# A new order of all engines' instructions, another bank map and another form of the mask in a fused decoder layer with a routed feed-forward part

## The reference

```
x = x + attn(layernorm(x))              # 16 heads of 8, no mask takes effect; attn itself adds its input again
x = x + xattn(layernorm(x), ctx, ctx)   # 16 heads of 64, RoPE on q and k,
                                        # scores * 64**-0.5, kept where (j <= i) & (j >= i - 32), else -1e30
x = x + ffn(layernorm(x))               # router picks 1 of 8 experts by argmax, plus a shared expert
# expert: silu(x @ gate.T) * (x @ up.T) @ down.T, hidden size 256
```

## Time and profile before

| | |
|---|---|
| median of three runs | 804.68 us (804.55 to 804.92) |
| profiled execution, its own time | 806.58 us |
| profiled execution, span from first to last instruction | 804.8 us |
| TensorE matmul busy | 760.4 us, 94% |
| VectorE busy | 531.7 us, 66% |
| ScalarE busy | 537.5 us, 67% |
| GpSimd busy | 536.5 us, 67% |
| mean busy share of the DMA engines | 25% |
| mean granted TensorE clock | 0.984 of full speed |

### The profile page before, as it was taken

The page is one execution under the profiler, slowest core; times in us unless marked ns, Lnnn a source line. Parts: engine busy times, 40 slices in busy tenths (PEclk is TensorE's granted clock), DMA queues, the critical chain, the costliest instruction groups (busy, mean ns, idle before and its releaser), DMA issues. The chain is left out here.

```text
span 804.8 us, 27623 instructions
## 1 busy us (share of the span) xinstructions
PE 760.4 (94%) x9852; PEld 623.1 (77%) x9852; DVE 531.7 (66%) x1350; ACT 537.5 (67%) x1900; POOL 536.5 (67%) x864
## 2 busy tenths in 40 slices
PE   4889999999999999999999999999899999998893
PEld 2668888888888888888888888888678777876552
DVE  3566776777777767777777767777866685555652
ACT  2367777777777777777777777777577566656451
POOL 4366777777777777777777777777575755565543
PEclk9799999999999999999999999999999999999997
DMA  6031233323222222221111122223150202333230
GB/s 234 8 119 64 91 91 91 91 83 90 89 91 71 70 72 71 70 68 59 60 58 58 67 71 71 71 71 127 68 151 3 81 24 83 103 102 105 69 101 12
DMA packets 56789, 64.01 MB, mean 80 GB/s; under 512 B 4015, under 2 KB 52917, under 8 KB 56657
## 3 DMA queue, kind: packets, MB, share of 16 engines
q1 hardware_dynamic: 52928, 54.06, 21.0%
q0 software_dynamic: 3008, 6.57, 2.4%
q10 hardware_dynamic: 720, 1.62, 0.5%
HBM read 17.79 MB, written 45.35 MB: 78 GB/s over the span
## 5 line engine op out<-in xcount | busy, mean ns | idle before, releaser
L789 ACT ACTIVATE PX<-P,mx 128x128 f32<-128x128 f32 x512 | 183.5, 409 | 67.5 <-DVE mx L559 67.5
L559 DVE TENSOR_REDUCE mx<-P 128x4 f32<-128x512 f32 x128 | 83.1, 674 | 155.4 <-PE P L298 155.4
L956 POOL TENSOR_TENSOR PX<-PX,mx 128x512 f32<-128x512 f32 x128 | 133.2, 1042 | 14.0 <-DVE mx L564 13.9
L789 ACT ACTIVATION_READ_ACCUMULATOR PX<-P,mx 128x1 f32 x512 | 127.2, 248 | 0.0
L951 POOL TENSOR_TENSOR rq<-rq,tq 128x1024 f32<-128x1024 f32 x32 | 75.6, 2363 | 60.5 <-DVE rq L523 60.5
L753 ACT ACTIVATE PS<-P 128x512 f32<-128x512 f32 x128 | 70.6, 607 | 24.9 <-PE P L219 24.9
L498 DVE TENSOR_REDUCE nmf<-P 128x4 f32<-128x512 f32 x128 | 81.3, 679 | 7.0 <-PE P L198 4.2
L798 ACT ACTIVATE PT<-P 128x512 f32<-128x512 f32 x128 | 76.5, 597 | 8.2 <-PE P L307 5.7
L307 PE MATMUL P<-c,PX 128*128 128x128 f32 x512 | 79.3, 278 | 0.0
L307 PEld LDWEIGHTS P<-c,PX 128*128 128x128 f32 x512 | 57.4, 142 | 24.1 <-issue 22.7
L946 POOL TENSOR_TENSOR rk<-rk,tk 128x1024 f32<-128x1024 f32 x32 | 75.5, 2359 | 0.0
(11 more groups left out here) (140 smaller groups left out, 1767.5 us busy)
## 6 DMA issues: line engine op xcount, KB each, us to landing
z_xs<-c SPq DMA_DIRECT2D x34, 1088.0 KB, 5.2
xrow<-z_xs SPq DMA_DIRECT2D x46, 136.0 KB, 3.3
ew<-in_ew SPq DMA_DIRECT2D x9, 384.0 KB, 3.8
x<-in_x SPq DMA_DIRECT2D x32, 64.0 KB, 1.8
cxT<-in_ctxT SPq DMA_DIRECT2D x31, 64.0 KB
out<-yst,xrow POOLq DMA_INDIRECT x46
wk<-in_wk SPq DMA_DIRECT2D x1, 512.0 KB, 4.5
wvT<-in_wvT SPq DMA_DIRECT2D x1, 512.0 KB, 7.1
```

The source lines that it names most:

```text
L559: dve.tensor_reduce(mx[b % 3][:, 0, r, :], v3(bank(f"ds{r}")), AX.X, ALU.max, negate=True).then_inc(S["v_dm"][r], 1)
L789: t = act.activation(PX[(4 * b + r) % 6][:, c, :], p[:, c * 128:c * 128 + 128], ACT.Exp, bias=m[:, 0, r, c:c + 1], scale=1.0, accum_out=m[ ...
L956: pool.tensor_tensor(X[:, :, :], X[:, :, :], mx[b % 3][:, 2, r, :].rearrange("p (h a) -> p h a", a=1).to_broadcast([128, 4, 128]), ALU.mul ...
```

## The change

Three things change. First, the order of the calls in the loops of all five engines; in part a stage is also moved to the turn before or after. The stages and what they compute stay as they are. Second, `BANK`, the map from slots to banks. Third, the mask of `d_s`: it is now written by slices of 32 keys. Sixteen matmuls (four slices for each of four banks) each multiply 32 rows of the transposed mask (`far`) with a 32 x 32 identity (`eye`), repeated for four heads, and write 128 x (4 x 32) elements. The constant `cb` grows from 1296 to 1328 columns.

The bank map and the mask:

```diff
-BANK = dict(a=2, cnt=5, dn=4, dpv0=4, dpv1=6, ds0=3, ds1=2, ds2=7, ds3=1, dt0=2, dt1=0, dt2=1, dt3=7, et=6, gu=0,
-            kE=3, kO=2, ln=7, nmt=2, oT=0, po=4, pos=0, qE=4, qO=5, qkv=1, rt=6, s0=7, s1=0, s2=5, s3=4, st0=5, st1=0,
-            st2=3, st3=6, v0=6, v1=1, wo=5, x1=3, xg0=5, xg1=4, xg2=3, xg3=0, xgt0=1, xgt1=2, xgt2=3, xr0=1, xr1=2,
-            xr2=7, xr3=0, xrt0=4, xrt1=5, xt0=3, xt1=4, xt2=7, xt3=6, xtt0=0, xy0=6, xy1=6, xy2=7, xy3=5, xyt0=6,
+BANK = dict(a=3, cnt=7, dn=1, dpv0=0, dpv1=3, ds0=0, ds1=3, ds2=4, ds3=1, dt0=7, dt1=1, dt2=0, dt3=2, et=6, gu=1,
+            kE=6, kO=6, ln=4, nmt=7, oT=2, po=6, pos=4, qE=3, qO=5, qkv=5, rt=6, s0=2, s1=3, s2=5, s3=0, st0=7, st1=6,
+            st2=2, st3=5, v0=2, v1=7, wo=7, x1=7, xg0=6, xg1=2, xg2=4, xg3=3, xgt0=1, xgt1=2, xgt2=3, xr0=1, xr1=5,
+            xr2=6, xr3=3, xrt0=4, xrt1=5, xt0=0, xt1=0, xt2=5, xt3=3, xtt0=0, xy0=2, xy1=2, xy2=1, xy3=7, xyt0=6,
             xyt1=7)
...
-        rows, cols = (cb[:, 784 + 256 * k:1040 + 256 * k].bitcast(BF16).rearrange("p (h n) -> p h n", h=2) for k in range(2))
+        far, eye = cb[:, 784:1296].bitcast(BF16).rearrange("p (w q) -> p w q", w=4), cb[:, 1296:1328].bitcast(BF16)
...
-                for h in range(2):
+                for w in range(4):
                     for r in range(4):
-                        pe.matmul(v3(p[r]), rows[32 * r:32 * r + 32, h, :],
-                                  cols[32 * r:32 * r + 32, h, :].rearrange("p (a k) -> p a k", a=1).to_broadcast([32, 4, 128]),
-                                  start=(h == 0), stop=False, skip_group_check=True)
+                        pe.matmul(v3(p[r])[:, :, 32 * w:32 * w + 32], far[32 * r:32 * r + 32, w, :],
+                                  eye[32 * r:32 * r + 32, :].rearrange("p (a k) -> p a k", a=1).to_broadcast([32, 4, 32]),
+                                  start=(w == 0), stop=False, skip_group_check=True)
```

On VectorE, in the part of the turn that the text speaks of:

```diff
+                batch(f_y, s - 8)
...
+                batch(b_max, s - 4, 1)
                 batch(b_max, s - 4, 2)
                 batch(b_max, s - 4, 0)
...
+                batch(f_pos, s - 8)
...
+                batch(r_q1, s - 5)
                 batch(r_q3, s - 5)
...
-                batch(d_max, s - 5, 2)
-                batch(f_pos, s - 7)
```

Before, `f_pos` is the last call of VectorE's turn, and `d_y`, `b_cn` and `f_y` open the next. On ScalarE the middle of the turn:

```diff
                 batch(b_nmT, s - 5)
+                batch(d_ox, s - 7, 0)
+                batch(d_ox, s - 7, 1)
+                batch(b_ps, s - 5, 0)
+                batch(b_ps, s - 5, 1)
+                batch(b_ps, s - 5, 2)
+                batch(b_ps, s - 5, 3)
+                batch(a_norm, s - 2)
                 batch(d_exp, s - 6, 1)
                 batch(b_oT, s - 5)
                 batch(d_exp, s - 6, 0)
+                batch(d_exp, s - 6, 3)
...
+                batch(a_q, s - 4)
                 batch(b_cnT, s - 5)
```

```diff
                 weights(s)
-                tile(next_r, s - 33, 0)
-                batch(clear, s - 6)
-                batch(first_r, s - 8)
-                batch(next_cx, s - 4)
+                batch(first_r, s - 9)
+                tile(next_r, s - 34, 0)
                 tile(next_r, s - 34, 1)
                 tile(next_r, s - 34, 2)
+                batch(next_cx, s - 4)
+                batch(next_x, s - 3)
                 tile(next_r, s - 34, 3)
-                batch(next_x, s - 2)
+                batch(clear, s - 6)
```

More of the change, by code:

```diff
@@ L68, in build @@
         c1 = sb("c1", [128, 646])
-        cb = sb("cb", [128, 1296], U16)
+        cb = sb("cb", [128, 1328], U16)
         c2 = sb("c2", [128, C2])
@@ L405, in _ @@
             for s in range(PERIODS):
[L406 to L414, removed]
-                batch(c_v, s - 4, 1)
-                tile(x_dn, s - 33, 1)
-                tile(x_up, s - 32, 0)
-                tile(x_hT, s - 33, 3)
+                batch(b_ln, s - 5)
@@ L419, in _ @@
+                batch(c_v, s - 4, 1)
+                tile(x_tr, s - 32, 2)
+                tile(x_dn, s - 33, 2)
+                batch(f_pos, s - 8)
+                tile(x_up, s - 32, 1)
+                batch(r_q, s - 5, 0)
+                tile(x_dn, s - 33, 3)
+                tile(x_hT, s - 32, 0)
                 batch(e_tr, s - 7)
[L420 to L423, removed]
+                batch(r_q, s - 5, 1)
@@ L424, in _ @@
+                tile(x_up, s - 32, 2)
+                batch(d_t, s - 6, 2)
+                tile(x_tr, s - 32, 3)
                 batch(f_up, s - 7)
[L425 to L434, removed]
@@ L435, in _ @@
-                batch(a_qkv, s - 3)
-                tile(x_dn, s - 33, 3)
                 batch(d_t, s - 6, 3)
                 tile(x_hT, s - 32, 1)
-                batch(b_st, s - 4)
+                batch(b_nm, s - 4)
                 batch(d_pv, s - 6, 0)
                 batch(d_pv, s - 6, 1)
+                batch(b_st, s - 4)
                 batch(d_s, s - 5)
                 batch(b_pv, s - 4)
-                batch(f_pos, s - 7)
+                tile(x_dn, s - 32, 0)
                 batch(d_wo, s - 6)
@@ L446, in _ @@
                 batch(b_oT, s - 4)
-                batch(f_dn, s - 7)
-                batch(r_k, s - 3, 1)
-                tile(x_dn, s - 32, 0)
+                batch(r_k, s - 3, 1)
+                tile(x_up, s - 32, 3)
+                batch(a_qkv, s - 3)
+                batch(b_cn, s - 4)
+                batch(c_v, s - 3, 0)
+                tile(x_hT, s - 32, 2)
+                tile(x_tr, s - 31, 0)
+                batch(a_tr, s - 1)
+                batch(b_x1, s - 4)
+                batch(f_dn, s - 7)
@@ L450, in _ @@
+                batch(r_k, s - 3, 0)
+                tile(x_dn, s - 32, 1)
+                tile(x_tr, s - 31, 1)
+                batch(d_t, s - 5, 0)
+                batch(d_t, s - 5, 1)
+                batch(b_s, s - 3)
+                tile(x_up, s - 31, 0)
+                tile(x_hT, s - 32, 3)
             for j in range(TILE0[1], NT + 4):
@@ L846, in _ @@
             for s in range(PERIODS):
[L847 to L855, removed]
-                tile(x_th, s - 33, 2)
-                tile(x_hT, s - 33, 0)
-                batch(b_nmT, s - 5)
-                batch(d_pt, s - 7, 1)
-                tile(x_xT, s - 33, 3)
-                batch(a_q, s - 4)
-                batch(d_pt, s - 7, 3)
-                tile(x_hT, s - 33, 1)
-                batch(b_ps, s - 5, 3)
-                batch(b_ps, s - 5, 1)
-                batch(b_ps, s - 5, 2)
+                batch(b_nmT, s - 5)
                 batch(d_ox, s - 7, 0)
@@ L1156 @@
     eye, b_in = np.eye(128, dtype=f), w["L0_attn_b_in"]
-    near = lambda q: (j <= q) & (j >= q - 32)
-    sets = [row[r::58] for r in range(58)] + [row[26 * r:26 * r + 26] for r in range(5)]
-    rows, cols = np.zeros((2, 64, 128), f)
-    for k, q in enumerate(sets):
-        rows[k, q], cols[k] = 1, np.where(near(q[:, None]).any(axis=0), f(0), f(-1e30))
-    four = lambda a: np.tile(a.reshape(2, 32, 128).transpose(1, 0, 2).reshape(32, 256), (4, 1))
+    seen = (row[None, :] >= row[:, None]) & (row[None, :] <= row[:, None] + 32)
+    far = np.tile(np.where(seen, f(0), f(-1e30)).reshape(4, 32, 128).transpose(1, 0, 2).reshape(32, 512), (4, 1))
     half = np.concatenate([eye, np.triu(np.ones((128, 128), f), 1), np.repeat(choose, 128, axis=1),
                            every([np.arange(8) * 128 * n for n in CHUNKS]) * (row[:, None] == 0),
-                           four(rows), four(cols)], axis=1).astype(f)
+                           far, np.tile(np.eye(32), (4, 1))], axis=1).astype(f)
     arrays["cb"] = (half.view(np.uint32) >> 16).astype(np.uint16)
```

98 lines of the change are left out of this document (55 added, 43 removed).

## The result

The changed kernel takes 818.85 us (median of 4 runs, 818.08 to 820.56). The kernel before takes 804.62 (four runs, the three that stand above and one of 802.64). The ratio is 1.0209, 95% interval 1.0183 to 1.0235: 2% slower, where 799.3 was forecast. One of the first experiment's ten executions took 2235 us, and its ratio leaves that one out. The profiled execution's own time is 818.08, its span 816.2, that is 11.4 longer than before.

A forecast was written before the change was run, and what follows sets the result against it. TensorE's queue plus its few waits was taken to bound the kernel. Turns -6.2, tile turns -1.0, first table +0.5 and tail +1.3 summed to -5.4 us: 799.3 us, forecast range 795.5 to 803, whole range 795.5 to 806.

The forecast's parts named there:

- Part 4: Start and end of the kernel: start 0, first table plus 0.5 us, SyncE's later issues free, end plus 1.3 us.
- The slower rival: `b_pv` waits 0.48 us, not 0.12, for ScalarE's exponentials each batch, bringing 810.8 us; chance 0.11.
- its point of 0.29: The `b_pv` wait in us, 0.12 + 5.4/32, from which waiting on the exponentials decides the result.
- The mask: TensorE's mask matmuls ahead of `d_s`: 0.33 us for 0.44, minus 0.11 a batch, bounds minus 0.22 and plus 0.03.
- The pairs do not bind: Judges a rival: the mask's sixteen weight-load and matmul pairs take 0.47 us or more, giving 803.8, no change; chance 0.08.
- The Trainium skill's figure: About 131 ns per 512-column pair, 81 per 128: mask 0.25 us dearer a batch, estimate 11.5 us higher; not adopted.
- The turn: One loop turn on TensorE: 0.11 + 0.08 + 0.07 = 0.26 us less, times 24 minus 6.2 us; expected 20.5 to 20.6.
- Part 3: TensorE's waits per turn: 0.30 us before, 0.23 after, minus 0.07, bounds plus 0.25 and minus 0.30; shared banks cost nothing.
- `b_x1` with 0.11: TensorE's wait at `b_x1` for ScalarE's copy `cnT`: 0.11 us a turn where 0.19 stood.
- The head: Order up to the first full turn keeps the same hand-offs: 0, plus or minus 2 us.
- The first `tile_table`: VectorE's first-chunk table: the 2.99 us wait moves from `b_cn` to before `d_s`, becoming 3.5; plus 0.5 us.
- The tail: Last `f_pos` 4.25 us later, scatter 2 us behind it, not 4.97, gaining 3.0; together plus 1.3 us.

The follow-up runs named there:

- the first experiment: The changed kernel with SyncE's clearing transfer, and the expert weights behind it, held until TensorE has finished that turn's `d_s`: 804.87 us, ratio 1.0018.
- the one-hot experiment: The changed kernel with VectorE's one-hot row compared from logits in PSUM with their maximum, the index operation removed: 827.3 us, ratio 1.0214.
- the last experiment: The kernel before with the new mask, `f_dn` and `f_y` ahead of `f_pos` for the last batch, first `tile_table` one turn later: 803.07 us, ratio 0.9947.

## Why the prediction was wrong

**The step that failed** is in Part 4: "SyncE's `next_x` and `clear` are issued up to a turn later; both have a turn of room." The room was measured against who waits for the data, and in that sense it was there: no wait on `x` or on the clearing appears. What the step left out is what the traffic does to others while it runs. It was costed at nothing; it costs 11.4 us of span between the two profiled executions and some 15 us by the ratios (the first experiment), and nothing else in the change is as large. No rival named it. It is not the whole miss: without the stalls the kernel is at 1.0018, where 799.3 would be 0.993, and the rest lies in the turn and the head below. The slower rival, `b_pv` waiting on the exponentials, did not decide: `d_s` advances 0.18 us more a turn, below its point of 0.29.

**The mask** was sized too small in the right direction: 0.22 us less a batch, where 0.11 was taken, at the lower bound that the prediction named. By itself it shortens the turn by 0.15, since `d_s` gives 0.06 back (the kernel with the mask alone). The pairs do not bind: sixteen take 14 ns each, less than L219's 21. The Trainium skill's figure (TensorE: Matmul & The Clock Gate, Back-to-back issue gap), which would have made the mask dearer, is not borne out here.

**The turn** was to be 20.5 to 20.6 and is 20.68. The new order gives 0 of the 0.15 it was to give: with the old mask the turn is 20.85 against 20.80. Part 3 let each shared bank come free "0.2 us or more ahead of its next user". Bank 1, which `gu` and `ds3` share, does not: its reader L592, behind the slow L583, ends at 323.01, 0.14 us ahead of the mask, in every steady turn, and with L583 short again the mask starts 0.25 us sooner (the one-hot experiment). But that wait is hidden: `b_pv` starts 2.76 us behind L219 with it and without it, and 2.82 with the old mask. So behind L219 the turn goes by the exponentials, which Part 3 had ready at 2.66, and the shorter mask brings `b_pv` forward by 0.06 us only. `b_x1` with 0.11 (0.22 for one pass of L184) is as predicted in ten of sixteen steady turns; in the others it doesn't wait.

**The head** was 0, plus or minus 2; it is 3.6 us by the third L207, before any stall. TensorE's timeline there:

```profile
41.62 1.17 PE L215 MATMUL P<-qT,KM 32*128 32x128 f32 x32 [0.97 <-DVE tq L523]
43.97 3.80 PE L298 MATMUL P<-rk,rq 32*128 32x128 f32 x64 [0.72 <-POOL rq L951]
```

"The same hand-offs" was wrong for `b_st` and `d_s`: they stand closer behind their producers. These two add up to 1.7 us. In the first 62 us TensorE is idle 20.3 us where it was 18.1, which leaves 1.4 of the 3.6. The clock can hold that much, though no run separates it: the granted clock is at 1.2 GHz for 17.1 us of the 62, where it was for 13.7, and in such a stretch (43.2 to 50.0) L298's 64 matmuls take 3.80 us, nearly twice the 2.03 of the steady turn.

**The first `tile_table`**: `b_cn`'s wait went, as said, and waits of nearly the same size came in the next turn, inside `d_pv` and ahead of `b_st`, one group before `d_s` (1.70 and 0.84 us in the change and in the first experiment). With 2.5 us where 3.5 was taken it is about right.

**The tail**: `f_pos` comes 4.3 us later against the last L329 (4.25 predicted), and from it to the first tile it is 9.40 us where it was 12.68: 3.3 less, 3.0 predicted. That the two agree is in part luck. The scatter starts 3.23 behind `f_pos`, not 2, since an `x_send` holds GpSimd at 766.62, and so brings 1.7 of the 3.0; the other 1.5 come between the scatter and the first tile (6.17 us for 7.71), which the prediction left as it was. Missed: TensorE then idles 2.68 us up to 770.89, and from 770.2 to 780.5 the granted clock is at 1.2 GHz, where the kernel before has no such stretch between 577.5 and 796.0. Pairs of L387 take 2.04 us in it for 1.12 at 2.4 GHz; the end loses 0.9 again.

In sum, for the spans: head +3.6, middle +7.1 (+9.6 of stalls with their clock, the rest the shorter turn), to the last L329 -1.2 (with two more stalls, of 1.45 and 0.84, in it), tail +1.0 and +0.9 of clock: +11.4.

## What to carry to other kernels

When bulk transfers are moved on a queue, ask also what else comes by DMA while they run: an engine's instructions do, and no semaphore shows it. Put megabyte transfers behind the stretch in which TensorE issues most instructions per microsecond, and hold them there with a wait on that stretch's own semaphore. One engine's order alone doesn't decide where the traffic falls (SyncE's new list alone: 1.0028), so read its place from the trace. And try a local change (here the mask, 0.5% faster by itself) without the reordering that comes with it. The reordering brought the stalls, and without them it still left the kernel at 1.0018 where the mask alone is at 0.995.

## What the runs showed of the hardware

**Instruction loads queue behind bulk traffic.** In the changed kernel 85 packets of 16 KB on the instruction queue q8 (1.39 MB) carry TensorE's program, one for every 256 of its instructions. With the DMA engines full, the packet at 88.9 us came 0.5 us behind the end of 1.5 MB of bulk traffic, and TensorE went on 2.1 us after it. It waited so seven times, 0.8 to 2.8 us each, five of them between the third L207 and the eleventh; with the clearing doubled, 44 us in all. The Trainium skill (Runtime: NRT & Kernel Launch, Instruction fetch mechanics) says that the sequencer fetches 16 KiB blocks over a DMA queue of its own, and that the cost of a crossing is mostly hidden. The trace agrees with block and queue; it does not agree with "hidden" for a stretch of 55 to 64 matmuls of 29 ns each behind 1.5 MB of traffic.

**A small VectorE instruction can take as long as GpSimd's large one.** VectorE and GpSimd of the changed kernel:

```profile
320.49 1.74 DVE L583 TENSOR_TENSOR OH<-c,lgu 128x8 bf16<-128x8 f32 x1
```

```profile
319.84 2.36 POOL L951 TENSOR_TENSOR rq<-rq,tq 128x1024 f32<-128x1024 f32 x1 [1.03 <-DVE tq L523]
```

The one ends at 322.23, the other at 322.20, and so it is, within 0.04 us, in 30 of the 32 turns; with one operand in PSUM it takes 0.17 us. By the Trainium skill (SBUF — State Buffer, SBUF: two separate sides) a VectorE instruction with two SBUF inputs and a GpSimd instruction that reads SBUF exclude each other, and the later one waits for the whole of the first: the trace agrees. It cost no time in the change, since `b_pv` waits for the exponentials either way. In the last experiment two instructions, one of them with a single tensor as input, lose 3.1 us in this way, ahead of a wait of 2.28 us on TensorE.
